# A two-layer decoder on one core: one add of the scan stage goes from VectorE to GpSimd, and three weight loads of the expert stage go behind the block rows

## The reference

```python
def _mamba(x, ...):                      # D_INNER = 256, D_STATE = 16
    xs, z = jnp.split(x @ W_in.T, 2, axis=-1)
    xs = silu(causal_conv(xs, conv_w, taps=4) + conv_b)
    dt, Bm, Cm = jnp.split(xs @ W_x.T, [8, 24], axis=-1)
    dt = jax.nn.softplus(dt @ W_dt.T + b_dt)
    dA, dBx = jnp.exp(dt[..., None] * A), dt[..., None] * Bm[:, :, None, :] * xs[..., None]
    # per token: h = dA_t * h + dBx_t;  y = sum over the states of h * C_t
    return (y + xs * D) * silu(z) @ W_out.T

def _L0_ffn_ref(x, Wg, W1, b1, W2, b2):  # 8 experts, the best 2 of each token
    probs = softmax(x @ Wg); topk_p, topk_i = top_k(probs, 2); topk_p /= topk_p.sum()
    return sum over k of topk_p[k] * (gelu(x @ W1[topk_i[k]] + b1) @ W2[topk_i[k]] + b2)

def _L1_ffn_ref(...):                    # 8 experts, the best 2; h = silu(x @ gate) * (x @ up)

x = x + _L0_attn_ref(_layernorm(x), ...)    # Mamba
x = x + _L0_xattn_ref(_layernorm(x), ctx_768, ...)
x = x + _L0_ffn_ref(_layernorm(x), ...)
x = x + _L1_attn_ref(_layernorm(x), ...)
x = x + _L1_xattn_ref(_layernorm(x), ctx_768, ...)
x = x + _L1_ffn_ref(_layernorm(x), ...)
```

## Time and profile before

| | |
|---|---|
| median of 3 runs | 1583.67 us |
| the profiled execution | 1580.65 us, span 1578.8 us, mean granted clock 0.88 |
| busy: TensorE, VectorE | 1227.9 us (78%), 1017.5 us (64%) |
| busy: ScalarE, GpSimd | 905.0 us (57%), 754.3 us (48%) |
| scan stage | 0 to 471 us |
| first expert stage | 758 to 930 us |
| second expert stage | 1394 to 1574 us |

### The profile page before, as it was taken

The page is one execution under the profiler, slowest core; times in us unless marked ns, Lnnn a source line. Parts: engine busy times, 40 slices in busy tenths (PEclk is TensorE's granted clock), DMA queues, the critical chain, the costliest instruction groups (busy, mean ns, idle before and its releaser), DMA issues. The chain is left out here.

```text
span 1578.8 us, 31345 instructions
## 1 busy us (share of the span) xinstructions
PE 1227.9 (78%) x11210; PEld 942.8 (60%) x11218; DVE 1017.5 (64%) x2383; ACT 905.0 (57%) x1718; POOL 754.3 (48%) x583
## 2 busy tenths in 40 slices
PE   6898989898768887765399947998698885528882
PEld 3666766676654665544299944666456663428771
DVE  5999999999997586655111117886379665423334
ACT  3988898889745775552255526776366453213333
POOL 2998899888844133444355541110113244335552
PEclk8999999999988788776599978999799777659996
DMA  5241222132000310111579734000200011146665
GB/s 188 82 140 55 109 82 83 55 109 82 28 1 17 45 39 29 39 42 54 160 235 263 228 83 82 16 15 16 74 2 24 24 32 34 31 140 201 197 199 175
DMA packets 98028, 138.51 MB, mean 88 GB/s; under 512 B 13965, under 2 KB 77402, under 8 KB 93684
## 3 DMA queue, kind: packets, MB, share of 16 engines
q1 hardware_dynamic: 85764, 117.08, 25.1%
q0 software_dynamic: 9088, 17.07, 3.2%
q10 hardware_dynamic: 3024, 2.36, 0.5%
HBM read 105.91 MB, written 28.19 MB: 85 GB/s over the span
## 5 line engine op out<-in xcount | busy, mean ns | idle before, releaser
L347 POOL TENSOR_TENSOR M_dbx<-M_u,M_b_sb 128x1024 f32<-128x1024 f32 x127 | 297.2, 2363 | 41.2 <-DVE M_e L433 16.4
L449 DVE TENSOR_TENSOR_SCAN M_h<-M_pA,M_dbx 128x512 f32<-128x512 f32 x256 | 297.7, 1203 | 3.4 <-ACT M_pA L609 3.1
L609 ACT ACTIVATE M_pA<-M_dt,M_a_neg 128x504 f32<-128x504 f32 x256 | 174.9, 684 | 33.4 <-DVE M_h L449 28.4
L2525 PE MATMUL X_bank<-F_xT,F_wbuf 128*128 128x256 f32 x624 | 151.2, 386 | 0.0
L1861 PE MATMUL X_bank<-L_ident,X_s_sb 128*128 128x128 f32 x512 | 96.9, 317 | 68.0 <-ACT X_pt_sb L1724 65.1
L2156 POOL DMA_INDIRECT F_slots<-F_line,F_pos x128 | 126.7, 990 | 43.0 <-issue 39.4
L1724 ACT ACTIVATE X_pt_sb<-X_bank 128x512 f32<-128x512 f32 x128 | 76.3, 596 | 112.3 <-PE X_bank L1861 112.3
L1549 DVE TENSOR_REDUCE X_smax<-X_bank 128x8 f32<-128x512 f32 x128 | 82.2, 683 | 89.0 <-PE X_bank L1852 87.2
L619 ACT ACTIVATE M_hc<-M_pT,M_cT 128x256 f32<-128x256 f32 x256 | 119.4, 467 | 33.3 <-PE M_pT L756 31.3
L772 PE MATMUL M_pY<-M_ident,M_hc 128*128 128x128 f32 x1024 | 136.7, 277 | 0.6 <-issue 0.2
L772 PEld LDWEIGHTS M_pY<-M_ident,M_hc 128*128 128x128 f32 x1024 | 126.6, 194 | 0.4
(11 more groups left out here) (338 smaller groups left out, 2811.0 us busy)
## 6 DMA issues: line engine op xcount, KB each, us to landing
M_b_sb<-M_rows_bc SPq DMA_DIRECT2D x32, 1024.0 KB, 4.8
F_wbuf<-in_F_wcat SPq DMA_DIRECT2D x39, 578.0 KB
F_wbuf<-in_F_wcat SPq DMA_DIRECT2D x39, 450.0 KB
X_s_sb<-F_slots SPq DMA_DIRECT2D x39, 132.0 KB
F_xblk<-F_slots SPq DMA_DIRECT2D x39, 132.0 KB
F_line<-F_line SPq DMA_DIRECT2D x16, 256.0 KB
S_ya<-F_answers SPq DMA_DIRECT2D x16, 256.0 KB, 6.1
F_slots<-F_pad ACTq DMA_DIRECT2D x16, 132.0 KB
```

What stands on the lines that cost most here:

```text
L347: pool.tensor_tensor(dbx[:, k % DBXS, :, :], u[:, g % 2, :, :], bc(b_sb[:, n, :], 1, 2), ALU.mult).then_inc(dbx_ready, 1)
L449: v.tensor_tensor_scan(h[:, k % STATES, half, :], pA[:, (2 * k + half) % DECAYS, :, :].rearrange("p b t -> p (b t)"), dbx[:, k % DBXS, hal ...
L609: act.activation(pA[:, (2 * k + half) % DECAYS, :, 1:SEQ], dt[:, g % 2, half, :].rearrange("p (b t) -> p b t", t=SEQ)[:, :, 1:SEQ], ACT.Ex ...
L2525: ins = pe.matmul(bank[:, H0 + 2 * (j % 2) + b, c % 2 * BLOCK:(c % 2 + 1) * BLOCK], wbuf[:, j % WBUFS, c * P:(c + 1) * P], xT[:, j % 2, :] ...
```

## The change

The add dt = lnv + relu of groups 1 to 7 is made by GpSimd, between its instructions soft_fix and the product of state 14; VectorE keeps it for group 0 alone (`first_dt`). In both expert stages SyncE issues the weights of two blocks, not five, ahead of the wait for the rows; the weights of blocks 2, 3 and 4 go right ahead of the rows of the same block. It reads the row addresses of two blocks, not three, ahead of the wait.

```diff
@@ gpsimd
+            def make_dt(g):
+                reach(pool, da_ready, 2 * (g - 1) * N)
+                pool.wait_ge(fix_ready, g + 1)
+                pool.wait_ge(relu_ready, 2 * g + 2)
+                pool.tensor_tensor(dt[:, g % 2, :, :], lnv[:, :, :], relu[:, :, :], ALU.add).then_inc(dt_ready, 1)
+
...
                 if n == 13 and c + 1 < GROUPS:
                     soft_fix(c + 1)
+                    make_dt(c + 1)
@@ vector
-                make_dt(0)
+                first_dt()
...
-            def make_dt(g):
-                reach(v, da_ready, 2 * (g - 1) * N)
-                reach(v, u_ready, g - 1)
-                v.wait_ge(fix_ready, g + 1)
-                v.wait_ge(relu_ready, 2 * g + 2)
-                v.tensor_tensor(dt[:, g % 2, :, :], lnv[:, :, :], relu[:, :, :], ALU.add).then_inc(dt_ready, 1)
+            def first_dt():
+                v.wait_ge(fix_ready, 1)
+                v.wait_ge(relu_ready, 2)
+                v.tensor_tensor(dt[:, 0, :, :], lnv[:, :, :], relu[:, :, :], ALU.add).then_inc(dt_ready, 1)
...
                     if n == 8:
                         rounding_of_1p(c + 1)
-                    if n == 12:
-                        make_dt(c + 1)
@@ expert_stage
+    EARLY_WEIGHTS = 2
...
         sp.wait_ge(d.table_ready, 1)
-        for j in range(WBUFS):
+        for j in range(EARLY_WEIGHTS):
             weights(j)
-        ahead = [first_row(j) for j in range(3)]
+        ahead = [first_row(j) for j in range(EARLY_WEIGHTS)]
         d.rows_written(sp)
         for j in range(XBUFS):
-            block_rows(j, ahead[j] if j < 3 else first_row(j))
+            if EARLY_WEIGHTS <= j < WBUFS:
+                weights(j)
+            block_rows(j, ahead[j] if j < EARLY_WEIGHTS else first_row(j))
```

## The result

| | before | changed |
|---|---|---|
| median (lowest to highest), us | 1584.03 (1583.32 to 1585.27), 4 runs | 1565.24 (1563.64 to 1568.61), 4 runs |
| ratio, 95% interval | | 0.9885 [0.9861, 0.9910] |
| profiled execution, span, us | 1580.65, 1578.8 | 1568.61, 1566.8 |
| mean granted clock in it | 0.880 | 0.887 |

Note first that the two profiled executions differ by 12.0 us only: that of before lies 3.4 us under its median, that of the changed kernel 3.4 us over its own. In the experiments further down, one run of the kernel before on chip C (1584.56 us) that fell into the slow state is left out of the means.

The account below looks back on a forecast made before the run. VectorE was taken to bound the scan stage, and the pad rows on ScalarE's queue to set the expert stages' start. Gains of 4.5 + 6.2 = 10.7 us off the 1583.67 us median gave 1573.0 us, range 1568.5 to 1580.0.

Parts of the forecast that it names:

- The add: Scan stage: seven adds leave VectorE, 8.0 us gross; late TensorE and ScalarE at group ends leave 4.5 us gain.
- The wait for decays: Scan stage: VectorE's wait for M_pA, 3.1 us before, was to grow to 6 or 7 us.
- TensorE is: Loaded group ends of scan stage: TensorE is late next, so its state 15 transposes come 0.25 us earlier, not 1.14.
- Rivals 1 and 4: Scan stage: VectorE's whole 8.0 us come out, 1569.5, 12%; or GpSimd late, gain gone or turned, 1577.5 or 1586.0, 5%.
- The transfers: Start of both expert stages: without three weight loads the last pad lands in 2.4 us; gain 3.7 and 2.5 us.
- Rival 2: Expert-stage starts: pads slowed by their own writing and the scatters, not the weights; transfers gain 0 to 1, 1578.5 us, 25%.
- the prediction's own sign of being wrong: Expert-stage starts: the prediction is wrong if the pads still land 5 us after issue.
- Rival 3: Blocks 2 to 8 of each expert stage: moved loads compete in the busy part, slower, 1589.1 us, 8%.
- The interleave: Expert stages behind the wait: weights between block rows cost nothing; where it fails, block 2 some 0.5 us late per stage.
- The sum: Whole kernel: 4.5 us from the add plus 6.2 us from the transfers, 10.7 us, median 1573.0 us.
- it would come to 1568.1 and 1569.9: Profiled execution: span 1578.8 us and time 1580.65 us, each less the full 10.7 us gain.

Follow-up runs that it names:

- silu runs: Kernel before and changed kernel, each with z's silu over one column of 512 in each half; one run each, scan stage 417.5 and 409.7 us.
- two adds of delay: Two 128x1024 VectorE adds after the last scan: in the kernel before, ratio 1.0047 (C), 0.9969 (D); in the changed kernel 0.9937 (B), 0.9942 (D) against before.

## Why the prediction was wrong

1. **The add: right.** Forecast 4.5 us, measured 4.9 on A and 5.2 on F, 5.2 alone on B. The wait for decays grew to 6.2 us (6 to 7 forecast), none for products came, and the adds cost GpSimd 2.36 us each, hidden. The prediction named TensorE as the first link of the chain ("TensorE is"), and ScalarE's wait of 0.61 us for its transposes is in the changed kernel's rows. The silu runs add that less work on ScalarE alone gives nearly the full 8 us back (7.8), so ScalarE's own work at the group's end was part of the price. Rivals 1 and 4 did not come.
2. **The transfers: right on A, with a term somewhat too small.** The gap was to shorten by 3.7 and 2.5 us; last pad to rows gave 4.3 and 3.1, since the pad lands in 1.75 and not 2.4 us. Rival 2 fell on A, where the pads got faster without the loads. On F they got faster too (the slowest from 8.0 to 5.8 us) but stayed slow, and the scatters end the gap, so there the prediction's own sign of being wrong, pads that still land 5 us after their issue, was met. Rival 3 fell: no expert stage is longer by more than scatter. The interleave was set at nothing, and no trace shows a cost of it: with either order block 2 is turned 6.6 to 7.1 us behind T in the first stage, and the second stage took 140.1 and 142.6 us on A with the old and new transfers, but 138.5 and 135.8 on B, and 117 to 121 on F.
3. **The sum: wrong.** It carried both gains to the end and left the stages between at their old length. The step that failed is the one from the scan stage to the expert stage: "it would come to 1568.1 and 1569.9" holds only if TensorE is granted the same clock behind a start 5 us earlier. In its place the runs show: in four traces on A, B and E with VectorE's add and no delay the first cross-attention took 300.1, 296.2, 296.8 and 299.2 us, in four with GpSimd's add 290.5, 286.9, 294.4 and 296.2: 298.1 and 292.0 in the mean, 6.1 ± 4.5 us, with 102 to 124 us at 1.2 GHz in place of 126 to 137. The stages that the edits touch give 12.3 us on A, 10.8 on E and 10.1 on F, where 18.8, 17.0 ± 4.5 and 15.7 ± 3.2 were measured: 5.6 to 6.5 us more each time.
4. **The profiled execution passed for typical.** The prediction met the span of the profiled changed kernel to 1.3 us (1568.1 for 1566.8), and there the agreement is luck: 9.6 us came in one stage and 8.9 went in later ones. Self- and second cross-attention took 452.5 to 474.2 us in eight traces on A, B and E, 465.6 in the mean with VectorE's add and 466.7 with GpSimd's, so their part is scatter and no effect of the change.

So the moment at which the attention starts orders the spells in all twenty traces, and the place of the add does not: with two adds of delay (in two of two traces) and with the shortened silu (in one each) the two kernels show each other's spells. What stays open is how much of the time this is. A band fixes the first 75 us of a stage of 290; the rest of it and the later stages scatter, and on chip C two adds of delay had the short spells in the trace and no gain in ten times. Nor is it shown why long and short spells alternate as they do, or why chips D and F are 100 us faster; the lower level lasts 90 instead of 137 us in F's first cross-attention, and queues issue faster, but the two were not parted.

## What to carry to other kernels

Work out a gain on the traces, but where TensorE is the bound of a later stage at a clock that changes, add a term for that stage: here one microsecond more at the 1.2 GHz level cost some 0.35 us in the first cross-attention (9.6 for 27.7), and a start 5 us earlier went with 20 us less of it in the first 75 us, while in two traces a start 1.4 us later than that took it back. Before explaining a difference, ask for the scatter of the kernel itself by stage: a stage that neither edit touches and that moved by 9 us is the place to look. And when work leaves the bound engine, what is next is read at the place where the load is largest: of 8.0 us 3.1 went to the chain of transposes, table loads and silus at the end of each group.

## What the runs showed of the hardware

- The granted clock of the same stretch can repeat from chip to chip nearly to the matmul (417 and 417, 518 and 516 matmuls in 75 us on A and F), and it changes with the moment at which the stage starts: 37.5 us of the lower level in 75 us with the last output projection 427.2 to 427.7 us behind the first scan, 13.7 to 20.5 us at 427.8 to 428.5, and such bands alternate from 417 to 431 us. The lower level begins as TensorE stands for 3.7 and 6.0 us between short pieces of work, or just behind it; in the kernel before it comes again for 20.5 us behind 30.7 us at the higher level in which TensorE was busy for 28.21, and in it TensorE is busy for 18.94.
- What the lower level costs is less than half its length. Span against time at the lower level, twice (1 - mean clock) x span, has within each kernel a slope of 0.39 on chips B, C and E, 0.34 on D and 0.30 on F (± 0.03 to 0.05). The Trainium skill (TensorE: Matmul & The Clock Gate, "Terms") puts the penalty at about the throttled time x (1 - K/N), that is 0.5 at half the clock. The runs of this kernel say 0.30 to 0.39; TensorE also waits in that time (it is busy 10.15 of 17.10 us in the first spell).
- Chips differ by 7 to 8% with one program, and the runs of it on each lie within 1.2 to 1.5%: 1582.5, 1569.2 and 1565.6 us on E, B and C, 1464.4 and 1465.3 on D and F. The scan stage, VectorE's, took 420.0 us on A and 420.2 on F; the rest made the difference.
- On chip F the eight pads are issued in 7.84 us and the slowest lands 8.0 us after its issue, 5.8 without three weight loads ahead; on A they are issued in 16.61 us and the last lands in 1.75 us without the loads, 4.87 with them (second stage).
- GpSimd's adds and VectorE's scans do not slow each other in a way that shows: the adds take 2361 ns (2373 for the equal subtraction), and the scans' median is 1209 ns with them in the kernel, 1202 without.
